# Attention with rotary keys on one Trainium2 core: exchanged halves of two heads in one product, the mask added by VectorE, a third buffer of rotated queries, and transposes one step later

## The reference

```python
B, Lq, Lk = (2, 512, 128)
H, HD = (16, 128)
KVC, QC, R = (64, 96, 64)
LOOKBACK = 8
def _rope(x, L):
    half = x.shape[-1] // 2
    ...
    x1, x2 = (x[..., :half], x[..., half:])
    return jnp.concatenate([x1 * cos - x2 * sin, x1 * sin + x2 * cos], axis=-1)
```

## Time and profile before

| | us |
|---|---|
| median of 3 runs | 2493.12 (2492.66 to 2495.16) |
| the profiled execution, its own time | 2496.72 |
| its span in the trace | 2494.9 |

### The profile page before, as it was taken

One profiled execution on the slowest core, in us unless ns is written; L12 is line 12 of the kernel. 1 busy time (PEld: TensorE's weight loads), 2 busy tenths in 40 slices (PEclk: granted clock), 3 DMA queues, 4 the chain that ended last, 5 costly groups with the idle time before them and its releaser, 6 DMA issues. The chain is left out here.

```text
span 2494.9 us, 44834 instructions
## 1 busy us (share of the span) xinstructions
PE 2177.7 (87%) x15430; PEld 1817.0 (73%) x15438; DVE 1842.8 (74%) x3709; ACT 1291.0 (52%) x3123; POOL 1243.8 (50%) x1697
## 2 busy tenths in 40 slices
PE   4969998599999989999987999979999983549996
PEld 2358887488888878888876888868888871327775
DVE  5866665599999989999986777764555548966775
ACT  1113332688888777888864333323444442436663
POOL 4913342699999878999973111103344341221112
PEclk9979999799999999999999999988999995869998
DMA  3201110200000110000004000010000000010001
GB/s 128 78 34 68 68 68 23 102 18 14 16 18 16 48 50 18 16 18 16 12 1 128 20 26 20 20 56 9 8 6 7 6 1 0 1 48 21 23 19 35
DMA packets 38639, 80.41 MB, mean 32 GB/s; under 512 B 5904, under 2 KB 25680, under 8 KB 34384
## 3 DMA queue, kind: packets, MB, share of 16 engines
q1 hardware_dynamic: 38416, 77.54, 9.4%
HBM read 64.94 MB, written 12.58 MB: 31 GB/s over the span
## 5 line engine op out<-in xcount | busy, mean ns | idle before, releaser
L1352 PE MATMUL bank<-l_wr,l_xq 128*128 128x256 f32 (+1 forms) x1024 | 216.3, 355 | 7.4 <-ACT l_raw L1461 7.4
L861 PE MATMUL bank<-m_xr,m_wgr 128*128 128x512 f32 x864 | 209.8, 391 | 1.4 <-DVE m_xr L980 1.4
L1687 POOL TENSOR_TENSOR l_tiny<-l_tiny,l_minus_half 128x6 f32<-128x6 f32 x128 | 176.4, 1378 | 10.7
L861 PEld LDWEIGHTS bank<-m_xr,m_wgr 128*128 128x128 f32 x864 | 157.6, 188 | 31.7 <-issue 2.0
L1352 PEld LDWEIGHTS bank<-l_wr,l_xq 128*128 128x128 f32 x1024 | 160.4, 194 | 25.6 <-issue 8.3
L1389 PE MATMUL bank<-l_wpr,l_cat 128*128 128x256 f32 x1024 | 168.5, 307 | 1.9 <-POOL l_cat L1738 1.9
L2031 POOL TENSOR_TENSOR l_pr<-l_pr,l_rowsum 128x512 f32<-128x512 f32 x64 | 66.5, 1040 | 205.7 <-DVE l_rowsum L1998 205.7
L1475 ACT ACTIVATE xn_T<-bank,l_head_b,l_head_w 128x512 f32<-128x512 f32 x128 | 99.6, 778 | 118.8 <-PE bank L1400 118.8
L1619 DVE TENSOR_TENSOR l_raw<-l_raw,l_tiny 128x768 f32<-128x768 f32 x128 | 159.0, 1242 | 0.1
L1367 PE MATMUL bank<-xn_T 128*128 128x128 f32 x1024 | 139.7, 280 | 18.2 <-ACT xn_T L1447 16.9
L1461 ACT COPY l_raw<-bank 128x512 f32<-128x512 f32 x256 | 140.1, 611 | 25.1 <-PE bank L1358 16.7
(11 more groups left out here) (327 smaller groups left out, 6266.0 us busy)
## 6 DMA issues: line engine op xcount, KB each, us to landing
l_stage<-in_l_w SPq DMA_DIRECT2D x8, 1024.0 KB, 4.8
l_centred<-l_stage SPq DMA_DIRECT2D x6, 1024.0 KB, 4.1
l_stage<-l_centred SPq DMA_DIRECT2D x6, 1024.0 KB, 4.8
m_unsplit<-in_m_w SPq DMA_DIRECT2D x14, 384.0 KB, 3.4
m_wg<-in_m_gu SPq DMA_DIRECT2D x18, 256.0 KB, 2.6
x_norm<-in_ctxT_b SPq DMA_DIRECT2D x32, 128.0 KB, 2.1
l_stage<-in_l_wp SPq DMA_DIRECT2D x4, 1024.0 KB, 4.9
l_saved<-l_xs SPq DMA_DIRECT2D x16, 256.0 KB, 2.0
```

Of the source, the lines that this page charges most:

```text
L861: r = e.matmul(banks[2 * (n % 2) + half][:, :], WGR[:, u % 2, a, k, half, :], XR[:, b, k, cols], start=k == 0 and m == 0, stop=k == KT - 1 ...
L1352: r = e.matmul(to, XQ[:, q % 2, v, k, :], WR[:, j, part, k, h0 * P:h1 * P], start=k == 0 and part == 0, stop=k == KT - 1 and part == 1)
L1687: pool_own.did(e.tensor_tensor(r0, var, minus_half[:, :], ALU.pow))
```

## The change

Rotary halves: of two neighbouring heads the even one keeps its rotary rows in partitions 64 to 127, and the odd one now has them in 0 to 63 (`WQ`, `cos` and the keys `KR` come in two arrangements, u = 0 and 1). `WS` then holds the exchanged halves of both heads in one 128-column product: 8 instead of 16. The key side gets a third small product instead of the second, and its adds work on 64 partitions each. The cosine product is written straight to `QR` (three buffers instead of two), and GpSimd adds the sine product in place, in two operations of 64 partitions x 256. The mask is fp32 and is added by VectorE while it takes the scores out of PSUM (`SM`); maximum and exponentials read `SM`. `score` now waits for that sum (`s_shown`) instead of the exponentials. Transposes, value products and output projection stand one step later. VectorE's order in a step is now rotary products, mask sum and maximum, reciprocal, x; GpSimd's is queries first, then probabilities.

```diff
@@ -1795,7 +1795,10 @@
-                    r = e.tensor_copy(WQ[0:QC, 8 * n:8 * n + 8, 0:C], banks[n][0:QC, :].rearrange("p (h c) -> p h c", h=8))
+                    to = WQ[0:QC, 8 * n:8 * n + 8, :].rearrange("p (a u) c -> p a u c", u=2)
+                    absorbed_part = banks[n][0:QC, :].rearrange("p (a u c) -> p a u c", a=4, u=2)
+                    for u in range(2):
+                        r = e.tensor_copy(to[:, :, u, u * C:(u + 1) * C], absorbed_part[:, :, u, :])
@@ -1848,9 +1852,9 @@
-                for weights, bank in ((WQ, pqa), (WS, pqb)):
-                    for h in range(4):
-                        r = e.matmul(bank[:, h * P:(h + 1) * P], weights[0:QC, 4 * (n % HG) + h, :],
+                for weights, bank, count in ((WQ, pqa, 4), (WS, pqb, 2)):
+                    for h in range(count):
+                        r = e.matmul(bank[:, h * P:(h + 1) * P], weights[0:QC, count * (n % HG) + h, :],
@@ -1866,14 +1870,13 @@
-                e.wait_ge(*s_qr(n + 1))
+                e.wait_ge(*s_qr(2 * n + 2))
                 e.wait_ge(*s_key(b + 1))
-                e.wait_ge(*s_mask(b + 1))
                 if n >= 1:
-                    e.wait_ge(*s_exp(n))
-                e.matmul(pscore[:, :], identb[:, :], four(mask[:, b % 2, :]), start=True, stop=False)
+                    e.wait_ge(*s_shown(n))
                 for h in range(4):
-                    r = e.matmul(pscore[:, h * P:(h + 1) * P], QR[:, n % 2, h, :], KR[:, b % 2, :], start=False, stop=h == 3)
+                    r = e.matmul(pscore[:, h * P:(h + 1) * P], QR[:, n % 3, h // 2, h % 2, :], KR[:, b % 2, h % 2, :],
+                                 start=True, stop=True)
@@ -1911,22 +1914,23 @@
-                e.matmul(pkv[:, 0:P], wkr[0:C, 0, :], KC[0:C, b % 2, :], start=True, stop=True)
-                e.matmul(pkv[:, P:2 * P], wkr[0:C, 1, :], KC[0:C, b % 2, :], start=True, stop=True).then_inc(s_krot.sem, 1)
+                for m in range(3):
+                    r = e.matmul(pkv[:, m * P:(m + 1) * P], wkr[0:C, m, :], KC[0:C, b % 2, :], start=True, stop=True)
+                r.then_inc(s_krot.sem, 1)
...
-                    if 0 <= s - 8 < N:
-                        out_project(e, s - 8)
+                    if 0 <= s - 9 < N:
+                        out_project(e, s - 9)
                     if 0 <= s - 5 < N:
                         score(e, s - 5)
+                    if 0 <= s - 8 < N:
+                        values(e, s - 8)
                     if 0 <= s - 7 < N:
-                        values(e, s - 7)
-                    if 0 <= s - 6 < N:
-                        turn_probs(e, s - 6)
+                        turn_probs(e, s - 7)
@@ -1976,10 +1980,13 @@
-                e.tensor_tensor(KR[:, j, :], pkv[:, 0:P], cosT[:, :], ALU.mult)
-                e.tensor_tensor(KS[:, j, :], pkv[:, P:2 * P], sinT[:, :], ALU.mult).then_inc(s_kro.sem, 1)
+                e.tensor_tensor(KR[:, j, :, :], pkv[:, 0:2 * P].rearrange("p (u t) -> p u t", u=2), cosT[:, :, :], ALU.mult)
+                e.tensor_tensor(KS[:, j, :], pkv[:, 2 * P:3 * P], sinT[:, :], ALU.mult).then_inc(s_kro.sem, 1)
                 e.wait_ge(*s_kro(b + 1))
-                e.tensor_tensor(KR[:, j, :], KR[:, j, :], KS[:, j, :], ALU.add).then_inc(s_key.sem, 1)
+                for u in range(2):
+                    rope = slice(C, 2 * C) if u == 0 else slice(0, C)
+                    r = e.tensor_tensor(KR[rope, j, u, :], KR[rope, j, u, :], KS[rope, j, :], ALU.add)
+                r.then_inc(s_key.sem, 1)
@@ -1991,19 +1998,35 @@
+                        e.tensor_tensor(QR[:, n % 3, :, :, :], pqa[:, :].rearrange("p (a u t) -> p a u t", a=2, u=2),
+                                        bc(cosT[:, :, :], 1, 2), ALU.mult)
+                        e.tensor_tensor(QB[:, n % 2, :, :], pqb[:, 0:2 * P].rearrange("p (a t) -> p a t", a=2),
+                                        bc(sinT[:, :], 1, 2), ALU.mult).then_inc(s_rot.sem, 1)
...
+                        e.tensor_tensor(SM[:, n % 2, :, :], split(pscore[:, :]), four(mask[:, n // HG % 2, :]),
+                                        ALU.add).then_inc(s_shown.sem, 1)
+                        e.wait_ge(*s_shown(n + 1))
+                        dve_own.did(e.tensor_reduce(negmax[:, n % 2, :], SM[:, n % 2, :, :], AXX, ALU.max, negate=True))
@@ -2011,32 +2034,27 @@
+                    n = s - 4
+                    if 0 <= n < N:
+                        e.wait_ge(*s_rot(n + 1))
+                        if n >= 3:
+                            e.wait_ge(*s_prob(n - 2))
+                        for u in range(2):
+                            rope = slice(C, 2 * C) if u == 0 else slice(0, C)
+                            e.tensor_tensor(QR[rope, n % 3, :, u, :], QR[rope, n % 3, :, u, :], QB[rope, n % 2, :, :],
+                                            ALU.add).then_inc(s_qr.sem, 1)
+                            e.wait_ge(*s_qr(2 * n + u + 1))
```

More of the change, by code:

```diff
@@ L1763, in l2_attention @@
             QCT = sb(scratch, "l2_qct", [P, 2, P])
-            mask = sb(scratch, "l2_mask", [P, 2, P], BF16)
+            mask = sb(scratch, "l2_mask", [P, 2, P])
             mtmp = sb(scratch, "l2_mtmp", [P, 2, 2, P])
-            QA = sb(scratch, "l2_qa", [P, 2, 4 * P])
-            QB = sb(scratch, "l2_qb", [P, 2, 4 * P])
-            QR = sb(scratch, "l2_qr", [P, 2, 4, P])
+            QB = sb(scratch, "l2_qb", [P, 2, 2, P])
+            QR = sb(scratch, "l2_qr", [P, 3, 2, 2, P])
+            SM = sb(scratch, "l2_sm", [P, 2, 4, P])
             negmax = sb(scratch, "l2_negmax", [P, 2, 4])
@@ L1913, in keys @@
                     e.wait_ge(*s_kro(b))
[L1914 to L1915 removed]
+                for m in range(3):
+                    r = e.matmul(pkv[:, m * P:(m + 1) * P], wkr[0:C, m, :], KC[0:C, b % 2, :], start=True, stop=True)
+                r.then_inc(s_krot.sem, 1)
             def tensor(e):
                 begin(e, ends)
[L1919 removed]
+                for s in range(N + 9):
                     if 0 <= s - 3 < N:
                         query(e, s - 3)
[L1922 to L1923 removed]
+                    if 0 <= s - 9 < N:
+                        out_project(e, s - 9)
                     if 0 <= s - 5 < N:
                         score(e, s - 5)
+                    if 0 <= s - 8 < N:
+                        values(e, s - 8)
                     if 0 <= s - 7 < N:
[L1927 to L1929 removed]
+                        turn_probs(e, s - 7)
                     if s % HG == 0 and s < N:
@@ L1945, in scalar @@
                 begin(e, ends)
-                for s in range(N + 8):
+                for s in range(N + 9):
                     n = s - 6
@@ L1998, in vector @@
                         e.reciprocal(rowsum[:, n % 2, :], rowsum[:, n % 2, :]).then_inc(s_inv.sem, 1)
[L1999 to L2004, removed]
-                        e.tensor_tensor(split(QB[:, n % 2, :]), split(pqb[:, :]), four(sinT[:, :]), ALU.mult).then_inc(s_rot.sem, 1)
-                    n = s - 8
+                    n = s - 9
                     if 0 <= n < N and n % HG == HG - 1:
@@ L2013, in vector @@
                         e.bn_stats(stats[:, b, :], X[:, b, :]).then_inc(bn.sem, 1)
-                    n = s - 5
-                    if 0 <= n < N:
-                        e.wait_ge(*s_score(n + 1))
-                        if n >= 2:
-                            e.wait_ge(*s_exp(n - 1))
-                        dve_own.did(e.tensor_reduce(negmax[:, n % 2, :], split(pscore[:, :]), AXX, ALU.max, negate=True))
-                        e.wait_ge(*dve_own.all())
-                        e.tensor_scalar(negmax[:, n % 2, :], negmax[:, n % 2, :], scale, None, ALU.mult).then_inc(s_max.sem, 1)
                     if s % HG == 1 and s < N:
@@ L2745, in layouts @@
     none = np.zeros((QC, H, C), np.float32)
-    L["l2_wq"] = np.concatenate([none, qr], 2)
-    L["l2_ws"] = np.concatenate([none, qr[:, :, swap]], 2)
+    odd = np.arange(H)[None, :, None] % 2 == 1
+    L["l2_wq"] = np.where(odd, np.concatenate([qr, none], 2), np.concatenate([none, qr], 2))
+    turned = qr[:, :, swap].reshape(QC, H // 2, 2, C)
+    L["l2_ws"] = np.concatenate([turned[:, :, 1], turned[:, :, 0]], 2)
     kr = I["L2_xattn_W_kr"]
-    L["l2_wkr"] = np.stack([np.concatenate([np.eye(C, dtype=np.float32), kr], 1),
-                            np.concatenate([np.zeros((C, C), np.float32), kr[:, swap]], 1)], 1)
+    eye = np.eye(C, dtype=np.float32)
+    L["l2_wkr"] = np.stack([np.concatenate(pair, 1) for pair in ((eye, kr), (kr, eye), (kr[:, swap], kr[:, swap]))], 1)
     half = C // 2
@@ L2754, in layouts @@
     cos, sin = np.cos(ang), np.sin(ang)
-    L["l2_cos"] = np.concatenate([np.ones((C, P)), cos, cos]).astype(np.float32)
-    L["l2_sin"] = np.concatenate([np.zeros((C, P)), -sin, sin]).astype(np.float32)
+    one = np.ones((C, P), np.float32)
+    L["l2_cos"] = np.stack([np.concatenate(rows) for rows in ((one, cos, cos), (cos, cos, one))], 1)
```

(1 more changed line is left out.)

35 lines of the change are left out of this document (21 added, 14 removed).

## The result

The changed kernel took 2468.01 us (median of 4 runs, 2463.43 to 2469.88) beside 2494.14 of the kernel before on the same chip (2492.66 to 2496.45). The ratio is 0.9892, with a 95% interval of 0.9875 to 0.9909. The profiled execution took 2469.88 with a span of 2468.1; before it was 2496.72 and 2494.9.

What follows compares the result with a forecast made beforehand. TensorE's stream was taken to bound the middle of the L2 attention stage. Its saving -39.5, waits +12.2 and drain +2.5 give -25 us: profiled 2496.72 becomes 2471.9, and the median, 0.14% below, 2468; range 2456 to 2481.

Steps and rivals of the forecast that it cites:

- The waits: After the keys, VectorE and GpSimd lock each other out; TensorE waits 0.41 and 0.40 us, 0.81 a batch, +12.2.
- rival A: Key rotation: the collision of VectorE and GpSimd costs nothing, nothing waits; -37, 2456 us; chance 0.23.
- 20.4 us: Length of one batch of four steps in the L2 attention stage, expected in the profile after the change.
- The saving of TensorE: TensorE's stream in L2 attention: 0.67 us less a step, 2.5 a batch, 39.5 in 16 batches without waits.
- The halves: GpSimd's two query adds of 64 partitions x 256: 0.72 us each, bounds 0.49 and 1.27.
- rival B: GpSimd's half adds cost 1.27 us each like the old whole; longer waits after the keys, +17, 2484; chance 0.11.
- rival C: GpSimd's half adds dearer still: gain used up at 1.47 us each; at 1.8, +11, 2504 us; chance 0.04.
- Rival D: Score path fails in ordinary steps (0.4 us margin): every step waits 0.1 to 0.2, 2474 to 2481 us; chance 0.07.
- The drain: Stage's end, from the start of the last scores, 9.6 us before: 2.5 us longer, bounds 0.7 and 4.
- The third buffer: Third buffer of rotated queries: keeps VectorE from waiting for the scores, worth nothing by itself.
- the later transposes: Transposes of probabilities one step later: give the score path a whole step more, needed where the maximum comes late.
- My 3.4: Time in a step when exponentials, reciprocal and scaling would be done in the old order, for transposes at 3.76.

Runs made afterwards that it cites:

- experiment 1: Changed kernel with VectorE's reciprocal of the row sums moved behind the key rotation: 2458.39 us, ratio 0.9851 to the kernel before.
- experiment 2: Changed kernel with the keys' sine product and two of the mask's three intermediate results kept in PSUM: 2459.75 us, ratio 0.9861 to the kernel before.
- experiment 4: Changed kernel with two buffers of rotated queries instead of three: 2490.8 us, ratio 0.9984 to the kernel before.
- experiment 7: Changed kernel with transposes, value products, copies, output projection and x one step earlier again, VectorE's order otherwise kept: 2727.54 us, ratio 1.0935 to the kernel before.
- experiment 3: Changed kernel with one more, unread GpSimd add of 64x256 in every step: 2474.31 us, ratio 0.9922 to the kernel before.
- experiment 8: Changed kernel with both the reciprocal behind the key rotation and the key rotation through PSUM: 2464.45 us, ratio 0.9879 to the kernel before.

## Why the prediction was right, and where it was off

**The number.** 2468 against 2468.01 is closer than the working deserves: the four executions lie between 2463.43 and 2469.88. The profiled execution was forecast at 2471.9 and took 2469.88, 2.0 less; but the median, which lay 3.6 below the profiled execution before the change, lies 1.9 below it now. The two misses cancel, which is luck. The stage became 27.2 us shorter where the sum said 24.8: its three terms, "-39.5 + 12.2 + 2.5", measure -39.1 (from the first keys to the last scores 317.0 in experiment 1, 356.2 before), +8.9 and +3.0. The waits were put 3.3 too high.

**The mechanism** was right in its steps: the batch shortens from 22.22 to 20.44, GpSimd's earlier work stands across the key rotation, and TensorE waits twice a batch, on the sine product and on `l_pt`. Experiments 1 and 2 confirm it from two sides, and rival A, in which nothing waits, is what experiment 1 measures, 9.6 us below. The "20.4 us" of the forecast, though, hit better than its own terms: 22.22 - 2.5 + 0.81 is 20.5.

**The saving of TensorE.** Forecast 0.67 a step, 2.5 a batch. Without waits the batch is 19.81 (experiment 1), so 2.41. The difference is the scores: they stayed at 0.98 to 0.99 and did not go to 0.97. The `ws` products gave 0.44 and the keys cost 0.23, as said.

**The waits.** Forecast "0.41" and "0.40", 0.81 a batch; measured 0.25 and 0.32, 0.57, and 0.64 with what follows the first. VectorE's side was right: mask done at 3.55 (3.48 forecast), sine product at 4.47 (4.53). On ScalarE's side two errors cancel: the copy is done at 3.53 of the next step, not at "3.40", since exponentials and copy take 2.11 (1747.60 to 1749.71) and not 2.01, and the values start 0.05 behind it and not "0.17", at 3.58 (3.57). The exponentials' extra price had been put at 0, "bound 0.03 each"; from start to start they are 0.39 apart here and 0.35 before, a little beyond the bound. TensorE's side was put too early. I had shortened the ordinary step of 4.93 to "4.26", but the step behind the keys lasted 5.04 before (1812.85 to 1817.89), and has 4.38 now (1741.56 to 1745.44, and 0.50). In the same way the values would have started at 3.26, not at "3.17". The term was +12.2 and is +8.9, as experiment 1 shows by taking it out. It also counted 15 batches; 14 have the waits. "Three or four" stretched operations are two and a trace of a third: the second add (0.85 for 0.29), the first mask operation (0.81 for 0.27), and the first add by 0.04, together 1.14 where "1.0" was written.

**The halves.** GpSimd's mean for 110 of them is 0.723 us against the 0.724 that I took from 128x256, which ends rivals B and C. A group by line of the changed kernel, 1720 to 2000:

```profile
L1944 ACT ACTIVATE l_pr<-l_sm,l_negmax 128x128 f32<-128x128 f32 x220 | 85.6, 391 | 36.4 <-DVE l_negmax L2024 36.4
L2050 POOL TENSOR_TENSOR l_qr<-l_qr,l_qb 64x256 f32<-64x256 f32 x110 | 79.6, 723 | 12.2
...
L2019 DVE TENSOR_TENSOR l_sm<-bank,l_mask 128x512 f32<-128x512 f32 x55 | 37.9, 689 | 30.1 <-PE bank L1878 30.1
```

The mask sum has its 0.689 in every step and no collision, and the values find `l_pt` in time in ordinary steps (the copy that starts at 1738.35 lasts 0.57; the values start at 1739.52). Rival D did not come.

**The drain** was put at "2.5, bounds 0.7 and 4". From the last scores (2013.91) to the last statistics' end (2026.46) it is 12.6, before 9.6: +3.0. With 16 batches of 1.78 less, that makes -25.5 of the -27.2 measured for the stage. The other 1.7 are not in the fill before the first keys, which come 6.0 us after the first context load in both kernels. From the first keys to the last (1687.94 to 1986.00, before 1687.43 to 2012.25) it is 26.8 less, and from there to the last scores 3.4 less: between the first keys and the last scores lie 67 steps, and 16 batches count 64.

**Two sentences were wrong, without harm to the sum.** The third buffer is not "worth nothing by itself": without it the change gains 4 us (experiment 4, 0.9984). I had asked only whether in-place sums need it, not when the cosine product of a group meets the scores that still read its buffer. And the later transposes are no safeguard for late maxima alone: with VectorE's new order, which puts the reciprocal behind mask sum and maximum, nearly every step waits 2.4 us without them (experiment 7). My 3.4 was worked out for the old place of the reciprocal, ahead of the rotary products; with that place it wasn't run.

## What to carry to other kernels

When a stream-bound engine gets shorter steps, list for the densest step of the cycle when each result of the others must be there, with the exact changeovers of that step, not those of the ordinary one: an error of 0.1 us a batch is a third of a wait. When an engine's work moves in time, look for what it will stand beside: GpSimd's adds cost nothing by load and 0.64 us a batch by their place, and moving a 0.17 us reciprocal was worth 9.6 us. A repair that works alone may not add to another, since each uses the same margin.

## What the runs showed of the hardware

A VectorE `tensor_scalar` from SBUF to SBUF with one tensor input is stretched by GpSimd's work just as a two-input operation is (0.81 for 0.27; 0.65 for 0.23 in experiment 3), down to the 128x4 scaling (0.53 and 0.61 for 0.17 in experiments 1 and 8); with its output in PSUM it isn't, but costs 0.35 instead of 0.27 for 128x128 (experiment 2). GpSimd's add of 64 partitions x 256 takes as long as that of 128 x 256 (0.723 us, and 0.724 in the earlier trace rows). ScalarE's exponentials of 128x128 take 391 ns from SBUF, where the kernel before had 364 from PSUM in the same stretch. And in experiment 7 waits of 2.4 us in every step were enough to bring the granted clock from 1.00 down to 0.78 over most of the stage, which made a loss of 9.5 us a batch into nearly 18.
